# Attention and a routed FFN on one core: another order for the last attention passes, and three places instead of two for the mixed tiles' weights

## Time and profile before

| | |
|---|---|
| median of 3 runs | 552.42 us (551.72 to 554.77) |
| the profiled execution | 547.5 us |
| its span, first to last instruction | 545.5 us |
| PE busy | 494.5 us, 91% |
| PEld, DVE, ACT, POOL busy | 435.1, 421.4, 353.8, 320.6 us |
| mean granted clock of TensorE | 0.953 |
| DMA | 83.72 MB, mean 153 GB/s |

### The profile page before, as it was taken

One profiled execution on the slowest core, in us unless ns is written; L12 is line 12 of the kernel. 1 busy time (PEld: TensorE's weight loads), 2 busy tenths in 40 slices (PEclk: granted clock), 3 DMA queues, 4 the chain that ended last, 5 costly groups with the idle time before them and its releaser, 6 DMA issues. The chain is left out here.

```text
span 545.5 us, 24637 instructions
## 1 busy us (share of the span) xinstructions
PE 494.5 (91%) x8593; PEld 435.1 (80%) x8593; DVE 421.4 (77%) x1117; ACT 353.8 (65%) x800; POOL 320.6 (59%) x570
## 2 busy tenths in 40 slices
PE   4579999999999999989897899898999999999890
PEld 3458888888888888878786689897999999999780
DVE  3437888898788885886886647899999999888583
ACT  3437777768686785674756487665667667677560
POOL 7801444445453464443526456788888888888584
PEclk9959999999999997997988999999999999999896
DMA  9697676787786968687567112222343266244510
GB/s 209 166 240 190 169 205 183 225 236 183 205 217 184 248 188 219 178 227 175 145 163 194 37 42 80 61 81 71 93 100 96 81 218 228 81 146 156 179 27 14
DMA packets 97353, 83.72 MB, mean 153 GB/s; under 512 B 37447, under 2 KB 88784, under 8 KB 97235
## 3 DMA queue, kind: packets, MB, share of 16 engines
q1 hardware_dynamic: 93874, 73.70, 49.7%
q0 software_dynamic: 3264, 8.41, 4.5%
q10 hardware_dynamic: 96, 0.04, 0.0%
HBM read 43.63 MB, written 23.62 MB: 123 GB/s over the span
## 5 line engine op out<-in xcount | busy, mean ns | idle before, releaser
L1683 PE MATMUL ps<-wo_hi,ks 128*128 128x256 f16 x576 | 129.5, 274 | 4.3 <-DVE ks L1269 4.0
L1701 PE MATMUL ps<-sT_hi,w_hi 128*128 128x128 f16 x496 | 104.9, 220 | 0.4 <-issue 0.4
L1701 PE MATMUL ps<-sT_lo,w_hi 128*128 128x128 f16 x496 | 105.0, 220 | 0.0
L1701 PE MATMUL ps<-sT_hi,w_lo 128*128 128x128 f16 x496 | 105.0, 220 | 0.0
L1146 DVE TENSOR_REDUCE mx<-ps 128x4 bf16<-128x512 f32 x128 | 82.7, 683 | 8.8 <-PE ps L1469 8.2
L666 POOL CAST att_hi<-att 128x256 f16<-128x256 f32 x32 | 12.7, 396 | 123.9 <-DVE att L974 123.9
L1683 PE MATMUL ps<-wo_lo,ks 128*128 128x256 f16 x288 | 78.8, 274 | 0.0
L816 ACT ACTIVATE probs<-ps 128x512 f32<-128x512 f32 x128 | 69.4, 612 | 6.6 <-PE ps L1495 5.9
L1372 PE MATMUL ps<-v_even,probs 128*64 128x17 f32 x1024 | 71.5, 212 | 1.4 <-issue 1.4
L1372 PE MATMUL ps<-v_odd,probs 128*64 128x17 f32 x1024 | 71.5, 212 | 0.3 <-issue 0.3
L1372 PEld LDWEIGHTS ps<-v_even,probs 128*64 128x64 f32 x1024 | 66.8, 141 | 5.1 <-issue 4.5
(11 more groups left out here) (266 smaller groups left out, 1531.4 us busy)
## 6 DMA issues: line engine op xcount, KB each, us to landing
qk_s<-qk_hi SPq DMA_DIRECT2D x64, 128.0 KB, 3.0
w_in<-in_L_ffn_W_dram SPq DMA_DIRECT2D x32, 256.0 KB, 4.0
v_odd<-slots SPq DMA_DIRECT2D x62, 128.0 KB, 2.1
qs<-qk_s SPq DMA_DIRECT2D x16, 384.0 KB, 4.3
ks<-qk_s SPq DMA_DIRECT2D x16, 384.0 KB, 5.2
ks<-qk_s SPq DMA_DIRECT2D x32, 144.0 KB, 3.9
v_even<-v_odd SPq DMA_DIRECT2D x63, 68.0 KB, 4.2
qk_s<-qk_lo SPq DMA_DIRECT2D x32, 128.0 KB, 3.5
```

Source lines behind the costliest of these rows:

```text
L1683: ins = mm(ps_y[p], h[p][hs][:, ic, :], wo[ws][:, ic, :], start=n == 0, stop=n == 3 * IC - 1)
L1701: up_ins = mm(ps_h[1 - p][:, half, col + m * width:col + (m + 1) * width], weights(ws, owners[m], k, ic), sT[1 - p][ss][:, k, at], start=k ...
```

## The change

On the last passes (`ending`: it from 28 to 31), TensorE does `values(1)` after the transposes of the maxima, and `turn_attention(done)` at the end of the pass (passes 28 to 30) into a bank of its own; in pass 31 the two parts of the first routed tile's product change places with it, and the turn and the projection of tile 30 come in step -1. DVE does the quotient after the chosen experts and the row statistics, and the copy of the turned tile after the slots. The early table is cut in three parts, of which those of passes 26 and 27 stand behind `qk_lo`; in pass 28 the table is written before `taken_early`.

The mixed tiles' weights have three sets of places (`COPIES`), each of single pieces of 2048 bytes per partition (`k` in range(CC), CC is 2), so that each DMA copies half of what one did. The first three mixed tiles' copies are issued in steps 20 to 25, one expert a step (four DMAs); the fourth's in steps 28 to 31, in four parts of two DMAs, the first after a wait on `h_done` of tile 28.

```diff
-        w1_mixed = [[[spare[4 * b + 2 * m + s] for s in range(2)] for m in range(PARTS_M)] for b in range(2)]
+        COPIES = 3
+
+        def w1_mixed(b, m, s, k):
+            return spare[((b * PARTS_M + m) * 2 + s) * CC + k]
...
+        ps_attT_next = ps[:, 0, 0:C].bitcast(f16).rearrange("p (s k t) -> p s k t", s=2, k=CC)
...
+        def attT_of(n):
+            return ps_attT if n + 1 < TILES - LEAD else ps_attT_next if n + 1 < LAST else ps_attT_last
...
                 for n in range(MIXED):
-                    m = j - (MIXED_AT[n] - (8 if n < 2 else 4))
-                    if 0 <= m < PARTS_M:
-                        if n >= 2:
-                            sp.wait_ge(h_done, 2 * MIXED_AT[n - 2] + 2)
+                    first = MIXED_AT[0] + (0 if n == COPIES else 2 * n - 8)
+                    steps = PARTS_M * 2
+                    per = 1 if n == COPIES else 2
+                    for c in range((j - first) * per, (j - first + 1) * per) if first <= j < first + steps // per else ():
+                        m, s = c // 2, c % 2
+                        if n == COPIES:
+                            sp.wait_ge(h_done, 2 * MIXED_AT[0] + 2)
                         else:
                             sp.wait_ge(slots_known, 3)
                             sp.wait_ge(w1l_done, TILES)
                             sp.wait_ge(y_done, TILES)
-                        no = entries(MIXED_AT[n])[m]
-                        owner = sp.value_load(expert[0:1, no:no + 1], min_val=0, max_val=E - 1)
-                        for s in range(2):
-                            sp.dma_start(w1_mixed[n % 2][m][s],
-                                         w1s[s][:, bass.ds(owner * CC, CC), :].rearrange("p u i -> p (u i)"))\
-                                .then_inc(mixed_ld[n % 2], 16)
+                        if c == (j - first) * per:
+                            no = entries(MIXED_AT[n])[m]
+                            owner = sp.value_load(expert[0:1, no:no + 1], min_val=0, max_val=E - 1)
+                        for k in range(CC):
+                            sp.dma_start(w1_mixed(n % COPIES, m, s, k),
+                                         w1s[s][:, bass.ds(owner * CC + k, 1), :].rearrange("p u i -> p (u i)"))\
+                                .then_inc(mixed_ld[n % COPIES], 16)
...
@@ DVE, a pass @@
-                if a_tile(done):
+                pair = old // 2
+                ending = it >= TILES - LEAD
+                if a_tile(done) and not ending:
                     quotient(done)
-                pair = old // 2
                 if a_tile(old) and old % 2 == 1:
                     chosen_expert(pair)
                 if a_tile(old):
                     row_stats(old)
+                if it == EARLY_OF + 4:
+                    early_table(it)
+                if ending:
+                    quotient(done)
...
                 if a_tile(old) and old % 2 == 1:
                     slots_of(pair)
-                if it == EARLY_OF + 2:
-                    early_runs()
-                    early_entries()
+                if ending:
+                    attention_turned()
                 if it == EARLY_OF + 4:
+                    write_table(0, 0, EARLY)
                     taken_early()
-                    write_table(0, 0, EARLY)
...
                         .then_inc(qkl_done, 1)
+                if it < EARLY_OF + 4:
+                    early_table(it)
...
@@ TensorE, a pass @@
                     if step == 3:
-                        wait(pe, attT_out, done + 1)
+                        wait(pe, attT_out, done if ending else done + 1)
...
+                ending = it >= TILES - LEAD
                 values(0)
                 scores(2)
                 scores(3)
-                values(1)
+                if not ending:
+                    values(1)
...
                     last.then_inc(mxT_done, 1)
+                if ending:
+                    values(1)
...
-                if it == LAST:
-                    first_up(first_owner, range(IC // 4, IC // 2))
-                elif a_tile(done):
+                if a_tile(done) and not ending:
                     turn_attention(done, ps_attT)
...
-                if it == LAST:
-                    turn_attention(done, ps_attT)
                 scores_t(2)
                 scores_t(3)
+                if ending and it < LAST:
+                    wait(pe, sl_done, it - TILES + 3)
+                    turn_attention(done, ps_attT_next)
+                if it == LAST:
+                    first_up(first_owner, range(IC // 4, IC // 2))
...
                 if j == -1:
-                    project(TILES - 2, TILES)
                     pe.wait_ge(exp_done, 4 * (TILES - 1) + 2)
                     first_up(first_owner, range(IC // 2, IC))
+                    pe.wait_ge(y_done, TILES - 2)
+                    pe.wait_ge(lg_done, TILES - 2)
+                    pe.wait_ge(place_done, TILES // 2 - 1)
+                    turn_attention(TILES - 2, ps_attT_last)
+                    project(TILES - 2, TILES)
```

More of the change, by code:

```diff
@@ L228, in attention_then_routed_ffn @@
         g = [g_even[:, :, :], g_odd]
-        spare = [ks[k][:, :, :, :].rearrange("p b h n -> p (b h n)")[:, (2 + n) * CC * I // 2:(4 + n) * CC * I // 2]
-                 for k in range(2) for n in (0, 2, 4)]
-        spare += [w1_in[:, :].bitcast(f16), wa_room[:, 0:CC * I // 2].bitcast(f16)]
-        w1_mixed = [[[spare[4 * b + 2 * m + s] for s in range(2)] for m in range(PARTS_M)] for b in range(2)]
+        spare = [ks[k][:, :, :, :].rearrange("p b h n -> p (b h n)")[:, (2 + n) * I:(3 + n) * I]
+                 for k in range(2) for n in range(6)]
+        spare += [w1_in[:, :].bitcast(f16)[:, n * I:(n + 1) * I] for n in range(2)]
+        spare += [wa_room[:, n * I // 2:(n + 1) * I // 2].bitcast(f16) for n in range(3)]
+        spare += [probs[:, n, :, :, :].rearrange("p i e q -> p (i e q)").bitcast(f16) for n in range(2)]
+        spare += [qk[k][s][:, :, :, :].rearrange("p w m n -> p (w m n)") for k in range(2) for s in range(2)]
+        spare += [wa[s][:, :, :].rearrange("p k n -> p (k n)")[:, 0:I] for s in range(2)]
+        COPIES = 3
+        def w1_mixed(b, m, s, k):
+            return spare[((b * PARTS_M + m) * 2 + s) * CC + k]
         h = [[ks[k][:, :, :, :].rearrange("p b h n -> p (b h n)")[:, s * IC * P:(s + 1) * IC * P]
@@ L294, in attention_then_routed_ffn @@
         vlow_ld = [sem(f"vlow_ld{k}") for k in range(2)]
-        mixed_ld = [sem(f"mixed_ld{k}") for k in range(2)]
+        mixed_ld = [sem(f"mixed_ld{k}") for k in range(COPIES)]
         w1_ld = [sem(f"w1_ld{k}") for k in range(2)]
@@ L1033, in whole_runs @@
                 link(nc.vector.tensor_scalar(runs[:, 0:E], tiles_f[:, :], -TO_WHOLE, None, ALU.add))
[L1035 to L1052, removed]
-                nc.vector.scalar_tensor_tensor(entry[0][:, 0:1], entry_no[:, :], float(P), entry[0][:, 0:1],
-                                               ALU.mult, ALU.add).then_inc(entries_known, 1)
+            def early_table(it):
+                if it == EARLY_OF + 2:
+                    dve.wait_ge(table_consts, 1)
+                    dve.wait_ge(place_done, EARLY_OF // 2)
+                    link(nc.vector.tensor_tensor(total[:, :], place[1 - EARLY_OF // 2 % 2][:, 2, :], region_at[:, :],
+                                                 ALU.subtract))
+                    whole_runs()
+                    link(nc.vector.tensor_tensor_scan(runs_to[:, 1:E + 1], ones_e[:, 0:E], runs[:, 0:E], 0.0, ALU.mult, ALU.add))
+                if it == EARLY_OF + 3:
+                    link(nc.vector.scalar_tensor_tensor(shift[:, 0:E], runs_to[:, 0:E], -float(P), begin[:, 0:E],
+                                                        ALU.mult, ALU.add))
+                    nc.vector.tensor_tensor(adds[:, 0, 0:E - 1], shift[:, 1:E], shift[:, 0:E - 1], ALU.subtract)
+                    link(nc.vector.tensor_scalar(passed[:, 0:E - 1], runs_to[:, 1:E], entry_no[:, :], None, ALU.is_le))
+                    link(nc.vector.tensor_tensor(added[:, :, 0:E - 1], passed[:, 0:E - 1].unsqueeze(1).broadcast_to([P, 2, E - 1]),
+                                                 adds[:, :, 0:E - 1], ALU.mult))
+                if it == EARLY_OF + 4:
+                    link(nc.vector.tensor_reduce(entry[0][:, :], added[:, :, 0:E - 1], AX.X, ALU.add))
+                    nc.vector.scalar_tensor_tensor(entry[0][:, 0:1], entry_no[:, :], float(P), entry[0][:, 0:1],
+                                                   ALU.mult, ALU.add).then_inc(entries_known, 1)
@@ L1662, in body3 @@
                         n = MIXED_AT.index(j + 1)
-                        pe.wait_ge(mixed_ld[n % 2], 16 * 2 * PARTS_M * (n // 2 + 1))
+                        pe.wait_ge(mixed_ld[n % COPIES], 16 * 2 * PARTS_M * CC * (n // COPIES + 1))
                         owners = list(range(PARTS_M))
@@ L1671, in weights @@
                     if j + 1 in MIXED_AT:
```

(2 more changed lines are left out.)

6 lines of the change are left out of this document (4 added, 2 removed).

## The result

The kernel after takes 566.11 us (median of 5 runs, 559.34 to 572.99) against 552.42 of before (549.75 to 554.77, 5 runs). The ratio is 1.022, with a 95% interval of 1.016 to 1.028: 12 us slower, 9 to 15 by the interval. Forecast were +7.3 us and a time of 559.7. The sign is right and the size was too small: against the stated 551 to 566 the median lies 0.1 us past the upper end, and 552.42 times the ratio, 564.5 us, lies inside. The profiled execution after, 572.0 us, is one of two that were over 1.5% above the fastest, so I read the places and the kinds of its waits from it, and sizes from the timed runs.

A forecast was written before the change was run, and what follows sets the result against it. It took TensorE to bound the routed part, with SP the hidden bound of its last sixteen steps. Attention's -1.1 us and the copies' +8.4 made +7.3, put on the 552.42 us median: 559.7 us, range 551 to 566.

The forecast's parts named there:

- The table's split: End of attention: the 1.77 us wait before pass 27's transposes and the low clock behind it go, -3.3 us.
- +1.4: Passes 28 to 30: 29.1 us in the new order against 27.7 measured before, one low-clock stretch included.
- +0.8: Pass 31 and what follows: tile 30's projection waits for DVE's copy, later maxima; +0.8 us (0 to +1.5).
- unexplained 1.36 us: TensorE's idle time inside pass 29's values product, with no releaser; the forecast left it in.
- the bound of +3.1: Passes 28 to 30: upper bound in us, if both low-clock stretches come as before.
- The copies: Routed part: more issues delay SP at step 31, and the whole shift reaches TensorE, +8.4 us (5.5 to 12).
- 0.53: SP's steps: assumed price in us of issuing one 256 KB copy, between bounds of 0.45 and 0.63.
- (a): Rival, routed part: the copies stay hidden since SP's pace follows bytes; 551 to 553.5 us, chance 0.17.
- (b): Rival, attention: passes 27 to 31 run at 2.4 GHz throughout without the stall, -5; about 548.5 us, chance 0.15.
- (c): Rival, routed part: waits at tiles 28, 29 and 33 drop the clock, +3 to +5 more; 563 to 565 us, chance 0.18.
- (d): Rival, attention: reordering doesn't shorten the passes, the only gain is at pass 27; inside the sum, no chance of its own.
- my -1.1 for attention: End of attention: sum of -3.3, +1.4 and +0.8 us, between about -4.5 and +2.5.

The follow-up runs named there:

- order_only: The kernel before with only the new order of passes 28 to 31, the early table whole in pass 26 as before: ratio 1.015.
- copies_only: The kernel before with only the change to the mixed tiles' copies (three places, 256 KB pieces, new steps of SP): ratio 1.011.
- split_only: The kernel before with each 512 KB copy issued as two of 256 KB in the same step, two places: ratio 1.015.
- three_whole: Against copies_only, same third place and schedule, but 16 whole copies of 512 KB instead of 32 of 256 KB: ratio 1.003 to the kernel before.
- table_only: The kernel before with only the early table cut in three parts, order of the passes and copies as before: ratio 0.995.
- passes_only: The kernel before with the new order of passes 28 to 31 and the early table in three parts, old copies: ratio 1.004.

## Why the prediction was right in sign and short in size

**The table's split** was put at -3.3 us and measured -2.8. Step right, the wait and the fall of the clock behind it included: on the average 6 us less at the low clock.

**The reordered passes** are where it failed: "+1.4" and "+0.8" together, for the step in which I "leave the unexplained 1.36 us in and one low-clock stretch of 3.4 us (1.7)". order_only measured +8.2. The reading of the waits was nearly right: those for `att_lo` shrank (3.9 us in copies_only, 1.1 in order_only), and waits for the maxima, `attT` and without a releaser came in smaller pieces. So was the reckoning of a pass at full clock: 8.9 us for pass 29, and 8.97 measured. What I set against it were passes of before with the low clock in them (10.15 and 9.43 us); at full clock the old one takes 8.35. And I carried over the clock of before, less one stretch. It is the largest term: +23 us at the low clock over the runs of order_only, 34 us in one piece in its profile. The sum should have had the low clock as an unknown with an upper end at the whole of the passes, since the earlier trace rows show the clock falling in just this stretch; the bound of +3.1 held only "both stretches as now".

**The copies** were +8.4 us (5.5 to 12) and measured +5.9 as a time (3.6 to 8.2), +9.4 in the profile's 33 steps. The mechanism is as written: more issues on SP, shown by split_only and three_whole. The price of an issue was off: the copies stand 0.61 to 0.69 us apart, about my upper bound of 0.63 and not at the 0.53 that I took (the lower bound was mis-added too: 396 ns and 0.1 make 0.50, not 0.45); one of 256 KB costs SP what one of 512 KB does. In steps 20 to 23 it hardly showed, since there the next load follows 1.6 us after the last copy's issue instead of 1.92 (446.65 to 448.57 in the earlier trace rows): a step with four copies is 0.98 us longer than one with two (7.21 and 6.23), where I had 0.85. In step 24 the next load came 3.9 us after the first copy (484.89 to 488.83), and I had 3.4. The waits came where they were put, at tile 28 (1.9 us) and at the end, "6 to 12 us" in all: 5.5 in the whole change's profile, 7.2 in copies_only's. In copies_only's 33 steps TensorE was idle for 12.6 us where it was for 5.8 before, and 5.1 of the 6.8 more are waits for loads. The remaining 2.6 of the 9.4 us are busy time for the same matmuls at the same mean clock of 0.99, which I can't explain. SP's waits for TensorE went too: from the first copies on they are 0.3 us instead of 1.0. (Before, SP also waited 0.6 us for POOL and 0.2 for DVE there, which "the rest it was issuing" leaves out.)

**The rivals.** (a), hidden copies, falls: three_whole and split_only copy the same bytes, with 16 issues in three places and 32 in two, and one is free, the other +8.4. The Trainium skill says that issue time is usually small beside the DMA's own ("DMA: Bandwidth & Descriptors", section "Issuing engines are not separate DMA queues"). Here it isn't: an issue takes 0.51 us, and 256 KB at the 422 GB/s of the earlier trace rows take 0.6 us (an estimate), and SP's pace follows the number of issues. (b), faster by the clock, falls for the whole change, though table_only's profile has what it asked for, passes 27 to 31 at 1.00 throughout. (Its -5 alone would be 547.4; the rest of its 548.5 has no term.) (c) named the right mechanism in the wrong place: the clock makes it slower still, and by about what the sum was short, but in attention's end and not at the waits for tiles 28 to 33, where the whole change had two stretches of 3.4 us, before one, and copies_only one. (d), that the passes don't get shorter, came true, and by both: the pass at full clock is 0.6 us longer, and the low clock costs more.

**The sum** as measured: -2.8 for the table, +8.2 for the order, +5.9 for the copies is +11.3, with about 12 (9 to 15) for the whole. Table and order together (passes_only) came out at +2.1 where their single values add up to +5.4, so the parts don't simply add: with the early split the low clock that the order brings is shorter, +12 us a run instead of +23. That my -1.1 for attention, with bounds of -4.5 and +2.5, holds the measured +2.1 is owed to this and so to luck: the sum had no term for it.

## What to carry to other kernels

Count issues, not bytes, on a queue that issues without pause: cutting 16 copies in two cost 8 us (5 to 12) with the same bytes, and taking a DMA of 1 KB out of each step, with its value load, paid for all of them. Where the trace of before shows the clock falling near the edit, smaller idle pieces aren't a gain by themselves: give the granted clock a term of its own, bounded by the whole stretch, and judge by its mean over many runs, since one profile has it by chance. And compare passes at the same clock: the old pass with its low stretch made the new one look shorter than it is. Change one of three things at a time: here the good third (the table's split) was hidden under two that lost.

## What was not expected of the hardware

- The granted clock read 0.50 (1.2 GHz) for 34 us in order_only and 41 us in the whole change, with TensorE busy for 97 and 96% of them. In the 4.0 us ahead of order_only's fall, at 296.0, TensorE was busy for 2.8 us, and its longest wait was 0.75 us. With 63 products of 128 columns more, 5.0 us of work, the clock read 1.00 in passes 28 to 30, and 0.50 for 6.8 us in pass 31. Why it fell and stayed down is open.
- Between the runs of one kernel a microsecond at the low clock went with 0.25 to 0.35 us of time, less than the half that the ratio of the two levels gives.
- SP's issue of a copy inside SBUF took 514 ns (median) for 256 KB, and 532 ns for 512 KB. Single issues took longer at either size, 1.32 us (step 25 of the whole change) and 0.84 us.
- The same copies issued by ACT removed every late load and lost 12 us against before: TensorE waited 7.2 us for DVE's half of the product instead.
